# A new placing of all steps in the hybrid block: usual batches, batch 0 and the last two batches

## What is computed

```python
x = L0_attn_a_x                                   # (16, 512, 256)
x = x + attn(layernorm(x))                        # 16 heads of 16, causal softmax, after an rmsnorm
x = x + ffn(layernorm(x))                         # base + shared + top 2 of 6 experts of rank 16
x = x + ssm(layernorm(x))
x = x + ffn(layernorm(x))

# ssm
xc = silu(conv(x, 4 taps)); delta = softplus(xc @ Wd.T + bd); Bm, Cm = xc @ Wb.T, xc @ Wc.T
decay = exp(A * dt)                               # 16 states for each of 256 channels
h = decay * h + dt * x * b; y = sum over states of h * c
out = (y * sigmoid(x @ Wg.T + bg)) @ Wo.T + bo
```

## Time and profile before

| | |
|---|---|
| median of 3 runs | 2007.66 us (2004.68 to 2013.28) |
| profiled execution | 2016.03 us, span 2014.2 us |
| busy share: PE, PEld | 87%, 52% |
| busy share: DVE, ACT, POOL | 86%, 70%, 56% |
| first scans of batch 1 | about 329 us |
| steady part, batches 1 to 12 in the scans | 330 to 1684 us |
| last gate of batch 15 | 1977 us |

### The profile page before, as it was taken

The page is one execution under the profiler, slowest core; times in us unless marked ns, Lnnn a source line. Parts: engine busy times, 40 slices in busy tenths (PEclk is TensorE's granted clock), DMA queues, the critical chain, the costliest instruction groups (busy, mean ns, idle before and its releaser), DMA issues.

```text
span 2014.2 us, 32842 instructions
## 1 busy us (share of the span) xinstructions
PE 1759.6 (87%) x10356; PEld 1054.9 (52%) x10356; DVE 1736.1 (86%) x3928; ACT 1402.5 (70%) x2724; POOL 1123.8 (56%) x933
## 2 busy tenths in 40 slices
PE   5789788988989898999989898989989898878875
PEld 3455454646556464646555464646555564535333
DVE  4554889999998999999998999999999989977782
ACT  2465767787776878787886878787877867664531
POOL 2000655666675565666676566756676655667330
PEclk8899989999999999999999999999999999988887
DMA  4222576776768686777768686876878686641110
GB/s 121 90 64 59 127 157 139 173 153 150 161 147 173 142 182 147 173 158 154 166 145 169 148 173 150 174 160 156 161 159 170 151 166 135 138 114 48 48 58 10
DMA packets 186094, 275.37 MB, mean 137 GB/s; under 512 B 33809, under 2 KB 125762, under 8 KB 185922
## 3 DMA queue, kind: packets, MB, share of 16 engines
q1 hardware_dynamic: 155682, 163.17, 31.7%
q0 software_dynamic: 30240, 110.11, 29.9%
HBM read 128.49 MB, written 34.08 MB: 81 GB/s over the span
## 4 chain that ended last, share of the span: by engine, by line
PE 30%; DVE 29%; DMA 16%; POOL 9%; issue 8%; ACT 6%; SPq 2%; POOLq 0%; DVEq 0%; ACTq 0%
DMA y<-hc 11%; DVE hc L1169 11%; DVE bank L1026 7%; PE bank L331 5%; PE bank L537 4%; POOL inp L1338 3%; DVE hc L1177 3%; POOL inp L1344 3%; PE bank L520 3%; DMA sk<-qk_parts 2%; PE bank L392 2%; PE bank L439 2%; PE bank L341 2%; PE bank L414 2%; PE bank L595 2%
## 5 line engine op out<-in xcount | busy, mean ns | idle before, releaser
L1169 DVE TENSOR_TENSOR_SCAN hc<-dec,inp 128x1024 f32<-128x1024 f32 x256 | 620.6, 2429 | 35.7 <-POOL inp L1344 18.3
L1026 DVE CUSTOM_DVE_ANT_0 bank<-bank,mask_qk 128x512 f32<-128x512 f32 (+3 forms) x1024 | 478.7, 507 | 87.3 <-PE bank L392 86.8
L1338 POOL TENSOR_TENSOR inp<-u,b_all 128x512 f32<-128x512 f32 x256 | 405.2, 1583 | 231.9 <-DVE hc L1169 116.2
L811 ACT ACTIVATE pt<-bank 128x512 f32<-128x512 f32 x640 | 377.8, 600 | 197.5 <-PE bank L416 196.2
L1344 POOL TENSOR_TENSOR inp<-u,b_all 128x512 f32<-128x512 f32 x240 | 391.0, 1629 | 18.8
L927 ACT ACTIVATE dec<-dt,a_neg 128x511 f32<-128x511 f32 x512 | 341.2, 724 | 52.0 <-DVE hc L1169 51.7
L1177 DVE TENSOR_TENSOR hc<-hc,bank 128x1024 f32<-128x1024 f32 x242 | 293.8, 1214 | 41.3 <-PE bank L574 40.7
L1351 POOL DMA_DIRECT2D y<-hc x210 | 184.9, 880 | 254.1 <-DMA y<-hc 132.7
L392 PE MATMUL bank<-sk,sq 96*128 96x512 bf16 (+3 forms) x1024 | 250.2, 306 | 71.2 <-DVE mall L1026 53.8
L414 PE MATMUL bank<-sq,sk 98*128 98x512 bf16 (+3 forms) x1024 | 272.1, 304 | 12.4 <-ACT pt L811 12.3
L392 PEld LDWEIGHTS bank<-sk,sq 96*128 96x128 bf16 x1024 | 89.2, 98 | 215.0 <-DVE mall L1026 88.7
(11 more groups left out here) (167 smaller groups left out, 3192.2 us busy)
## 6 DMA issues: line engine op xcount, KB each, us to landing
y<-hc POOLq DMA_DIRECT2D x210, 512.0 KB, 5.3
b_all<-b_kept SPq DMA_DIRECT2D x256, 256.0 KB, 3.8
qk_parts<-parts SPq DMA_DIRECT2D x96, 256.0 KB, 3.4
sq<-qk_parts SPq DMA_DIRECT2D x384, 64.0 KB, 3.5
sk<-qk_parts SPq DMA_DIRECT2D x384, 64.0 KB, 3.6
X<-in_x SPq DMA_DIRECT2D x16, 512.0 KB, 6.8
out<-X SPq DMA_DIRECT2D x16, 512.0 KB, 3.7
sq<-hlt SPq DMA_DIRECT2D x256, 2.0 KB
```

The costliest lines, as they stand in the source:

```text
L811: A(pt[:, n % PT, :], score_bank[unit % 2][:, :], ACT.Exp).then_inc(exp_done.sem, 1)
L1026: return V.tensor_tensor_reduce(src[:, o:o + n], src[:, o:o + n], mask_qk[:, T - n:T], 1.0, -3.0e38, ALU.add, ALU.max, out)
L1169: V.tensor_tensor_scan(h, d, v, 0.0, ALU.mult, ALU.add).then_inc(scan_done.sem, 1)
L1338: first = G.tensor_tensor(inp[:, n % 2, 0, :], u[:, 0, :], b_all[:, k % 3, :], ALU.mult)
```

## The change

The tables of all five engines get new numbers for the usual batches. A table OWN beside them has places of their own for batch 0 (kind 1), batch 14 (kind 2) and batch 15 (kind 3), since these have other work around them. `by_batch` makes of each place a tuple of four, one for each kind, and `due` looks up the kind of the batch. Three entries of BANK change. No operation is added, removed or resized, and each engine issues as many instructions as before. The lines of the kernel after are those of before plus 88.

```diff
-             "gate": (145, 144), "bc": (149, 150, 154), "dt": (147, 149), "x3": (249, 251), "turn1": (258, 258),
+             "gate": (144, 144), "bc": (149, 150, 154), "dt": (148, 149), "x3": (249, 251), "turn1": (258, 258),
...
-            "x1": (0, 1), "turn0": (1, 1), "low0": 1, "hw0": 0, "up0": (0, 1), "xs": (0, 1), "conv": (0, 0),
-            "gate": (0, 1), "bc": 1, "dt": (0, 0), "x3": (1, 0), "turn1": (0, 1), "low1": 1, "hw1": 0, "up1": (0, 1)}
+            "x1": (0, 1), "turn0": (1, 1), "low0": 1, "hw0": 0, "up0": (1, 0), "xs": (0, 1), "conv": (0, 1),
+            "gate": (0, 1), "bc": 1, "dt": (0, 0), "x3": (1, 0), "turn1": (1, 0), "low1": 1, "hw1": 0, "up1": (0, 1)}
...
-    SP_AT = {"parts": (-44, 4), "load_x": -112, "store_b": 153, "store": 278, "stack": (-29, -31, -31), "maxima": -7,
+    SP_AT = {"parts": (-42, 5), "load_x": -113, "store_b": 153, "store": 286, "stack": (-27, -30, -31), "maxima": -7,
...
+    OWN = {
+        1: {
...
+            "SP": {"parts": (-35, -7), "load_x": -118, "store_b": 151,
...
+    KIND = [1 if a == 0 else max(a - NB + 4, 0) if a >= NB - 2 else 0 for a in range(NB)]
+
+    def by_batch(engine, usual):
+
+        rows = [{**usual, **OWN[k].get(engine, {})} if k else usual for k in range(4)]
+        return {key: tuple(zip(*(row[key] for row in rows))) if isinstance(usual[key], tuple) else
+                tuple(row[key] for row in rows) for key in usual}
...
-            a, rest = divmod(now - at, FRAME)
-            return a if rest == 0 and has(a) else -1
+            for kind, place in enumerate(at):
+                a, rest = divmod(now - place, FRAME)
+                if rest == 0 and has(a) and kind == KIND[a]:
+                    return a
+            return -1
```

More of the change, by code:

```diff
@@ L106, in hybrid_block @@
-    ACT_AT = {"res": (-30, -29), "square_f": 99, "square_s": 126, "square_l": 252, "norm_f": 103, "norm_s": 130,
[5 rows of a table removed]
-              "decays": (154, 162, 166, 170, 170, 177, 188, 190, 198, 201, 208, 213, 213, 218, 221, 224)}
-    DVE_AT = {"gated": 245, "add_x3": (250, 250), "in0": 112, "in1": 264, "out0": 115, "out1": 271,
-              "add_up1": (277, 278), "add_x1": (93, 95), "add_up0": (123, 125), "silu": 142, "delta": 153,
-              "stats_q": -111, "finish": -9, "heads": 28,
-              "scan": (158, 169, 169, 171, 178, 185, 191, 194, 200, 207, 211, 215, 217, 224, 228, 232),
-              "product": (162, 170, 173, 176, 183, 190, 193, 195, 203, 209, 214, 216, 220, 226, 231, 234)}
@@ L118, in hybrid_block @@
-    POOL_AT = {"rsqrt_f": 87, "rsqrt_s": 131, "rsqrt_q": -108, "rsqrt_l": 237, "low": (103, 261),
-               "inputs": (147, 152, 152, 152, 157, 166, 170, 176, 201, 205, 209, 213, 214, 215, 216, 225),
-               "add": (160, 152, 160, 169, 177, 181, 190, 203, 209, 212, 213, 214, 216, 225, 225, 227)}
-    SP_AT = {"parts": (-44, 4), "load_x": -112, "store_b": 153, "store": 278, "stack": (-29, -31, -31), "maxima": -7,
-             "load_b": (153, 155, 157, 160, 167, 171, 177, 180, 181, 192, 198, 208, 215, 220, 220, 222)}
+    PE_AT = {"res": (-30, -29), "xn": (-75, -72), "qk00": (-56, -51, -50), "qk01": (-47, -45, -44),
[6 rows of a table added]
+             "sum": (161, 168, 175, 180, 189, 192, 197, 200, 205, 209, 212, 219, 224, 228, 231, 235)}
@@ new lines, in hybrid_block @@
+    DVE_AT = {"gated": 247, "add_x3": (250, 250), "in0": 112, "in1": 262, "out0": 114, "out1": 271,
+              "add_up1": (276, 279), "add_x1": (92, 94), "add_up0": (125, 126), "silu": 144, "delta": 153,
+              "stats_q": -110, "finish": -9, "heads": 27,
+              "scan": (158, 169, 169, 171, 177, 183, 191, 194, 200, 207, 211, 215, 219, 224, 229, 232),
+              "product": (161, 170, 173, 179, 186, 190, 192, 199, 205, 210, 214, 216, 220, 227, 231, 236)}
+    POOL_AT = {"rsqrt_f": 86, "rsqrt_s": 129, "rsqrt_q": -108, "rsqrt_l": 236, "low": (114, 261),
+               "inputs": (148, 151, 152, 154, 161, 164, 169, 176, 197, 204, 206, 213, 214, 215, 216, 223),
+               "add": (160, 154, 161, 167, 177, 184, 192, 198, 206, 212, 213, 214, 219, 226, 227, 228)}
@@ new lines, in hybrid_block @@
+    KIND = [1 if a == 0 else max(a - NB + 4, 0) if a >= NB - 2 else 0 for a in range(NB)]
[3 more added lines that the diff above has]
+                tuple(row[key] for row in rows) for key in usual}
+    PE_AT, ACT_AT, DVE_AT, POOL_AT, SP_AT = (by_batch(engine, usual) for engine, usual in (
+        ("PE", PE_AT), ("ACT", ACT_AT), ("DVE", DVE_AT), ("POOL", POOL_AT), ("SP", SP_AT)))
@@ L246, in due @@
         def due(now, at):
-            a, rest = divmod(now - at, FRAME)
-            return a if rest == 0 and has(a) else -1
+            for kind, place in enumerate(at):
[3 more added lines that the diff above has]
+            return -1
         def group(now, at):
-            g, rest = divmod(now - at, HALF)
+            g, rest = divmod(now - at[0], HALF)
             return g if rest == 0 and 0 <= g < NQ else -1
```

44 lines of the change are left out of this document (42 added, 2 removed), and 52 rows, old and new, of tables (ACT_AT, OWN, PE_AT).

## The result

Sixteen executions of the changed kernel have a median of 2019.03 us, sixteen of the kernel before 2006.67 us; the ratio is 1.0057 (95% interval 1.0039 to 1.0075). The change costs 12 us, 0.6%. I had forecast 1990 us, 18 us less. The time lies outside the range of 1968 to 2016 and on the wrong side.

The account below looks back on a forecast made before the run. DVE was taken to bound the steady part, PE close behind. Steady batches -12 us (0.9 per batch, 13 batches), batch 0 -2 and handover -4 gave -18, so 2007.7 to 1990 us; own range 1980 to 2001, 8-in-10 range 1968 to 2016.

Parts of the forecast that it names:

- (4): Steady batches: product and head_norm swaps, later silu, `up0` ahead of maxima, shifted B loads; 0.4 us per batch lost, worst 0.5.
- The rival of the convolutions: Convolutions come too early, DVE waits for the units behind both; 2022 us, period 114 us, chance 0.13.
- (1): Steady batches: earlier spread of C for state 13 on PE, softplus one exp earlier; 0.9 us per batch won, bounds 0.3 and 1.6.
- (2): Steady batches: scan 12 one unit of maxima later, POOL's sum of state 6 earlier; 0.7 us per batch won, bounds 0 and 1.1.
- (3): Steady batches: two convolutions one unit of scores forward on PE; 0.3 us per batch lost, bounds 0 and 1.8.
- The ends: Outside the steady part: -2 us in batch 0, -4 us at batches 14 and 15 with the end of the last batch.
- The handover: To batches 14 and 15: head_norm and turn earlier, turn up to 4.5 us sooner; taken -4 us, bounds -6 and -1.
- Batch 0: Store of Q and K parts issued earlier, stack some 2 us sooner for PE's third group; taken -2 us, bounds -3 and 0.
- the ends go wrong: Batch 0: first group's scores start some 5 us later, behind the store; about 1998 us, no chance of its own.
- the first one: Rival that waits only change places: only 0.3 us per batch arrives, eaten by (3) and (4); 2001 or 2002 us, chance 0.29.
- The rival that PE has room: DVE alone is the bound; waits of (1) and (2) go in full, covers of (3) hold; 1967 us, chance 0.14.

Follow-up runs that it names:

- run 2: Kernel after with scan 4, product 3 and product 7 of the usual batches back at 178, 176 and 195 on DVE: 2009.53 us, ratio 1.0010.
- run 17: Kernel of run 5 with scan 4 of the usual batches one unit of maxima later still (180 instead of 178): 1983.70 us, ratio 0.9892.
- run 6: Kernel before with only scan 4 at 177, product 3 at 179 and product 7 at 199: 2017.35 us, ratio 1.0057.
- run 3: Kernel after with softplus of the usual batches back one exp later on ACT (151 instead of 150): 2018.13 us, ratio 1.0064.
- run 7: Kernel before with only the spread of C for state 13 earlier (226) and scan 12 one unit of maxima later (219): 1995.02 us, ratio 0.9939.
- run 10: Kernel of run 7 with softplus one exp earlier on ACT (150 instead of 151): 2029.89 us, ratio 1.0129.
- run 4: Kernel after with both convolutions of the usual batches back one unit of scores later on PE and ACT: 2023.16 us, ratio 1.0090.
- run 11: Kernel of run 7 with both convolutions one unit of scores earlier on PE (135, 138): 1999.68 us, ratio 0.9964.
- run 14: Kernel of run 7 with the first FFN's up-projection and its adds moved later (123, 125 and 125, 126): 2000.41 us, ratio 0.9963.
- run 1: Kernel before with only the own places of batches 0, 14 and 15 from the kernel after: 2041.81 us, ratio 1.0182.
- run 8: Kernel after with batch 0 at the places of the usual batches: 2022.53 us, ratio 1.0072.
- run 15: Kernel after with scan 4, products 3 and 7, softplus, convolutions and up-projection with its adds all back: 2031.66 us, ratio 1.0122.
- run 5: Kernel after with the edits of run 2 and run 3 together (scan, products and softplus back): 2010.19 us, ratio 1.0017.

## Why the prediction was wrong

**The step that failed** is the premise of the whole sum, "so no busy time is removed; only waits can move". The waits moved nearly as forecast, DVE's idle time over twelve batches fell by 7.5 us, and its busy time rose by 25.1, since scans that meet POOL's multiplies last longer (28.7 us). The places where this happens, scan 4 from 178 to 177, product 3 from 176 to 179 and product 7 from 195 to 199, are not in the list of moves above; in the sum they can only be among the product swaps of (4), priced at a wait of at most 0.5 us per batch, all of (4) at 0.4. Taking them back wins 9.5 us (run 2), and with softplus back the next place of scan 4 is worth another 26 us (run 17). The trace of before had the warning: a scan of 2.29 us in the earlier trace rows, and a mean of 2423 ns. I priced moves by the waits in the list, and a meeting of DVE and POOL is no wait: it hides in the durations. How much of the 9.5 us is the meetings and how much PE's wait behind the later products stays open (runs 2 and 6).

A second term failed too: softplus was counted as a gain of 0.6 us per batch, "It does by one exp on ScalarE". I looked at who waits for softplus and not at who waits for the exp that it was put in front of. In the kernel after the gain is there (delta_u waits 1.0 us instead of 6.4 in run 3) and PE's wait of 26.2 us beside it; together they are worth nothing that can be measured. On the kernel of run 7 the same move costs 35 us (run 10).

**Right by luck.** The rival of the convolutions had 2022 us, a period of 114 us and a sign, maxima that wait 2 us or more per batch for PE. Measured are 2019 us, 114.35 us and 40.5 / 12 = 3.4 us. All of it came, and the cause is another: putting the convolutions back wins nothing (run 4). The sign doesn't tell this rival from others. Nor do the 22 us that run 17 wins confirm the forecast of 18; they are not its terms.

**Point by point.** (1) and (2) together: forecast 0.9 + 0.7 us per batch, 21 us; without the 0.6 of softplus, which run 7 doesn't move, 1.0 per batch or 13 us (the 1.3 per batch in the expectation of run 7 doesn't go with its 13 us). Measured 12 us (run 7), 9 of them by (2) alone, forecast 9; for (1) alone 4 were forecast and 2 measured, with an interval from a gain of 7 to a loss of 4. The slack of delta_u was the next late thing, with 0.5 us per batch. (3) forecast +4 us, measured 5 (run 11), and (4) forecast +5, measured 5 for its up-projection alone (run 14); neither can be told from nothing, since the intervals overlap with run 7's. The ends: forecast -4 for the last two batches, and from the first scan of batch 13 to the end 326.5 us against 330.4. Over all traces the median of this stretch is 325.5 us with the new places of the last two batches (run 1 left out) and 328.4 with the old. The handover itself (DVE, then PE), beside the earlier trace rows:

```profile
1804.59 2.29 DVE L1257 TENSOR_TENSOR_SCAN hc<-dec,inp 128x1024 f32<-128x1024 f32 x1 [1.72 <-POOL inp L1432]
...
1808.80 0.25 DVE L1150 RECIPROCAL rc<-bank 128x16 f32<-128x16 f32 x1
```

```profile
1809.57 0.66 PE L413 MATMUL bank<-ident,ao 128*128 128x128 f32 x4 [1.14 <-DVE ao L1152]
```

The turn comes 5.0 us behind the first scan of batch 14, 9.7 before: 4.7 us sooner, where the prediction had up to 4.5. The end comes 3.9 us sooner in these two executions; how much of that the handover makes is not shown.

**Batch 0**: forecast -2, nothing measured. PE's wait changed its place. The scores of the first group wait for the stacked maxima, which SP issues behind the store, and the third group then starts 0.6 us later than in the earlier trace rows:

```profile
62.53 0.61 PE L502 MATMUL bank<-sq,sk 98*128 98x512 bf16 x1 [4.85 <-DMA sq<-hlt]
...
69.57 0.39 PE L480 MATMUL bank<-sk,sq 96*128 96x512 bf16 x1 [0.16 <-DMA sk<-qk_parts]
```

The prediction had this in its last rival ("the ends go wrong") and counted it with the first one. Run 8, without batch 0's own places, is 3.5 us slower, with overlapping intervals.

**The rival that PE has room** had both waits of (1) and (2) go in full, 35 us; run 7 has 12. But that is no verdict on the share of weight loads, 755 of 1354 us (56%) in the kernel after as before. In run 2 DVE stands idle 74.3 us for PE, and PE in its turn waits 35.4 us for the exp and 17.2 for the tokens: it is held up by ScalarE and POOL, which says little about its room. The rule of the Trainium skill ("Perfetto Trace Analysis", "Identifying the Most-Contended Engine"), that MFU and this share, and not the busy time of the matmuls, tell how much room TensorE has, is neither borne out nor refuted by a run here.

**What stays open.** The single moves don't add up. Two moves -12, convolutions and up-projection +5 each, the ends -4: that would be -6, and the kernel of run 17, which has all of them, scan 4 at 180 and softplus as before, is 22 us below the kernel before. Some 16 us come from places that no run separated, scan 4's own at 180 among them: it was never tried on the kernel of run 7. Nor is the path settled by which the three places of DVE lose 9 us in run 6, or why four moves put back make the kernel slower (run 15).

## What to carry to other kernels

Where two engines exclude one another, a meeting costs something whichever side loses, and the side that wins can carry it into the next one. The kernel where scan 4 loses 1.8 us (run 3, 2018 us) and the one where a step of 0.2 us in front of TensorE's work loses 2.1 (run 5, 2010 us) are both far slower than the one where neither does (run 17, 1984 us). Before moving a block on a queue, ask who waits for the instructions that it is put in front of, not only who waits for the block; and read durations beside waits, over the same batches and not over a fixed stretch of time, since a blocked instruction shows as a long one. With two engines near 90% and above, an edit that removes one cause may give little (run 2: 34 us of DVE's busy time, 9.5 us of time) because the other engine is late next, so a small result of a single undoing doesn't clear its suspect.

## What was not expected of the hardware

A vector product of 128x4 numbers on GpSimd took 0.20 us undisturbed and 2.28 us beside a VectorE scan of 2.29 us, so here the length of the block came from the other instruction and not from its own size. A scan that met one half of POOL's inputs took 4.06 us, and the other half then 3.15 instead of 1.27 us. Which side lost turned on tenths of a microsecond and less, and with it on places elsewhere in the program; the start in the trace alone doesn't tell it. The norm's step lost when it started 0.01 us behind the scan and won 0.09 us ahead of it, but scan 4 of the kernel after lost although its start is 0.35 us ahead of that of POOL's multiply.
